# A four-layer decoder on one core: when and from which queue layer 0's expert weights are loaded

## The reference

```python
logits = x @ router_weight.T + router_bias            # [4096, 16]
top_val, top_idx = top_k(logits, 4); softmax(top_val)
gate_up = einsum('th,ehd->etd', x, gate_up_proj) + gate_up_proj_bias   # 256 -> 512 per expert
gate, up = gate_up[..., ::2], gate_up[..., 1::2]      # clipped at 7
out = einsum('etd,edh->eth', (up + 1) * gate * sigmoid(1.702 * gate), down_proj) + down_proj_bias
```

## Time and profile before

| | |
|---|---|
| median of 3 runs | 3678.72 us (3677.7 to 3682.36) |
| profiled execution, first to last instruction | 3689.2 us |
| phase_norms to the end of phase_experts0 | 588 to 1435 us of it |
| TensorE busy over the whole span | 2870.5 us (78%) |
| DMA over the whole span | 386.10 MB, mean 105 GB/s |

### The profile page before, as it was taken

One profiled execution on the slowest core, in us unless ns is written; L12 is line 12 of the kernel. 1 busy time (PEld: TensorE's weight loads), 2 busy tenths in 40 slices (PEclk: granted clock), 3 DMA queues, 4 the chain that ended last, 5 costly groups with the idle time before them and its releaser, 6 DMA issues. The chain is left out here.

```text
span 3689.2 us, 60303 instructions
## 1 busy us (share of the span) xinstructions
PE 2870.5 (78%) x20178; PEld 1835.6 (50%) x20178; DVE 2185.6 (59%) x4954; ACT 1479.2 (40%) x3032; POOL 1095.9 (30%) x1490
## 2 busy tenths in 40 slices
PE   5388884476699995559957698999989649999993
PEld 4223332332355553423323486454568538888782
DVE  7689993577577776634468687888868620000003
ACT  5267772154222224659945454222245211111110
POOL 2111110177233335512269543000034441111110
PEclk7599996599899997569978899999989659999996
DMA  8766644299522223378600252000044221111204
GB/s 261 177 116 119 122 107 140 69 367 361 175 80 80 79 81 133 128 126 128 114 1 1 91 170 65 1 1 1 1 140 143 87 62 56 48 55 50 85 28 137
DMA packets 261609, 386.10 MB, mean 105 GB/s; under 512 B 56865, under 2 KB 188942, under 8 KB 261056
## 3 DMA queue, kind: packets, MB, share of 16 engines
q1 hardware_dynamic: 234480, 312.50, 31.7%
q0 software_dynamic: 25152, 68.22, 5.3%
q10 hardware_dynamic: 1680, 1.57, 0.2%
HBM read 227.49 MB, written 160.24 MB: 105 GB/s over the span
## 5 line engine op out<-in xcount | busy, mean ns | idle before, releaser
L3125 POOL DMA_INDIRECT rows_out<-e_out,e_tr_dest x224 | 234.9, 1048 | 875.9 <-DVE e_out L3755 514.1
L1195 ACT ACTIVATE a_pt<-a_psS 128x512 f32<-128x512 f32 x512 | 277.5, 595 | 155.5 <-PE a_psS L1093 151.1
L3755 DVE COPY e_out<-e_psD 128x512 f32<-128x512 f32 x40 | 27.7, 692 | 496.3 <-PE e_psD L3723 496.1
L1217 DVE TENSOR_REDUCE a_mx_sb<-a_psM 128x4 f32<-128x1024 f32 x256 | 293.1, 1215 | 18.9 <-PE a_psM L1076 17.7
L3523 PE MATMUL e_psG<-e_wgu,e_yT 128*128 x576 | 275.1, 600 | 25.8 <-ACT e_yT L3551 23.2
L1107 PE MATMUL a_psV<-a_pt,a_vt 128*18 128x256 f32 x4096 | 292.2, 387 | 2.0 <-issue 1.6
L3723 PE MATMUL e_psD<-e_w,e_hT 128*128 128x256 f32 x1280 | 293.3, 389 | 0.0
L3712 PE MATMUL e_psH<-e_yT,e_w 128*128 128x256 f32 x1280 | 285.4, 381 | 1.6 <-issue 0.8
L3655 ACT ACTIVATE e_hT<-e_psH 128x512 f32<-128x512 f32 x160 | 95.5, 597 | 456.4 <-PE e_psH L3712 453.1
L3723 PEld LDWEIGHTS e_psD<-e_w,e_hT 128*128 128x128 f32 x1280 | 248.2, 196 | 34.2
L3712 PEld LDWEIGHTS e_psH<-e_yT,e_w 128*128 128x128 f32 x1280 | 244.8, 191 | 35.8 <-issue 2.1
(11 more groups left out here) (428 smaller groups left out, 6110.2 us busy)
## 6 DMA issues: line engine op xcount, KB each, us to landing
kbd<-e_bgu SPq DMA_DIRECT2D x64, 512.0 KB
cr_kbd<-kbd SPq DMA_DIRECT2D x64, 512.0 KB, 3.4
rows_in<-zeros POOLq DMA_DIRECT2D x36, 522.0 KB, 6.6
e_xin<-rows_in SPq DMA_DIRECT2D x144, 128.0 KB
vbd<-e_bd SPq DMA_DIRECT2D x64, 272.0 KB
cr_vbd<-vbd SPq DMA_DIRECT2D x64, 272.0 KB, 2.7
cq_rows<-rows_out SPq DMA_DIRECT2D x32, 512.0 KB, 5.9
e_w<-in_L_ffn_w_dram SPq DMA_DIRECT2D x16, 1024.0 KB, 7.6
```

The costliest lines, as they stand in the source:

```text
L1195: act.activation(pt[:, probs(t, h), b, :, :], psS[:, unit(t, h, b) % S_BANKS, :].rearrange("p (k c) -> p k c", k=KC), ACT.Exp, scale=scale ...
L1217: dve.tensor_reduce(mx[:, t % 2, :, h, :], psM[:, k % 2, :, :].rearrange("p b (f c) -> p b f c", f=2), AX_X, ALU.max).then_inc(ring_read, 1)
L3125: pool.indirect_dma_start(out=self.rows_out[0:limit, :], out_offset=bass.IndirectOffsetOnAxis(ap=self.dest[:, t:t + 1], axis=0), in_=rows, ...
```

## The change

- `phase_norms` issues no loads any more.
- `phase_project` issues the router's weight and bias first, and behind them on the same queue `load_up`: the 16 loads of the first weights and the load of the first bias (12 MB).
- `KeysValues` uses the room of the second weights `e_wd` (seen as [128, 16, 512]) in place of the first bias's room; the second bias's room as before.
- `late` is gone from `phase_scatter`. At the start of `phase_experts0` ScalarE's queue issues `load_down`: the second weights in four loads of four experts each (1 MB, 1,024 pieces of 1 KB), and the second bias (2 MB), before ScalarE's first copy.
- TensorE and VectorE wait at the start for the first weights and bias alone; TensorE waits for all of `e_wd` before its first product with it, VectorE for the second bias before its first addition of it.

```diff
-def phase_norms(core, name, prefetch=None):
+def phase_norms(core, name):
...
-            if prefetch is not None:
-                @block.sync
-                def _(sp):
-                    prefetch(sp)
...
@@ phase_project
                     sp.dma_start(b[:, :], bias.rearrange("(a n) -> a n", a=1).broadcast_to([P, E])).then_inc(bias_loaded, 16)
+                if prefetch is not None:
+                    prefetch(sp)
...
@@ phase_scatter
                     pairs.sync(sp)
-                    late(sp)
...
+class Experts0:
+    PARTS = 4
...
+    def rooms(self):
+        return self.wd[:, :, :, :].rearrange("p e k d -> p e (k d)"), self.bd
...
+    def load_up(self, sp):
+        for e in range(self.E):
+            sp.dma_start(self.wgu[:, e, :, :], self.gate_up[e].rearrange("(k p) f -> p k f", p=P)).then_inc(self.up_loaded, 16)
+        sp.dma_start(self.bgu[:, :, :], self.gate_up_b.rearrange("(a e) f -> a e f", a=1).broadcast_to([P, self.E, self.D2])).then_inc(self.up_loaded, 16)
...
+    def load_down(self, eng):
+        n = self.E // self.PARTS
+        for m in range(self.PARTS):
+            eng.dma_start(self.wd[:, m * n:(m + 1) * n, :, :],
+                          self.down[m * n:(m + 1) * n].rearrange("e (k p) d -> p e k d", p=P)).then_inc(self.down_loaded, 16)
+        eng.dma_start(self.bd[:, :, :], self.down_b.rearrange("(a e) f -> a e f", a=1).broadcast_to([P, self.E, self.D])).then_inc(self.bias_loaded, 16)
...
@@ phase_experts0
-                pe.wait_ge(loaded, 16 * (2 * E + 2))
+                pe.wait_ge(weights.up_loaded, 16 * (E + 1))
...
                         pe.wait_ge(h_copied, t + 1)
+                        if t == 0:
+                            pe.wait_ge(weights.down_loaded, 16 * weights.PARTS)
...
             @block.scalar
             def _(act):
+                weights.load_down(act)
...
-                dve.wait_ge(loaded, 16 * (2 * E + 2))
+                dve.wait_ge(weights.up_loaded, 16 * (E + 1))
...
                         dve.wait_ge(down_done, t + 1)
+                        if t == 0:
+                            dve.wait_ge(weights.bias_loaded, 16)
```

More of the change, by code:

```diff
@@ L450, in _, with phase_project @@
                 pool.wait_ge(powed, 1)
-def phase_project(core, name, E, result, weight_rows=None, weight_cols=None, bias=None, yT_all=None, squares=None):
+def phase_project(core, name, E, result, weight_rows=None, weight_cols=None, bias=None, yT_all=None, squares=None, prefetch=None):
     nc = core.nc
@@ L2749, in _, with phase_scatter @@
                 c.link(dve.tensor_copy(slot[:, :, :], pos[:, :, :]))
-def phase_scatter(core, name, K, slot, rows_in, limit, mark, prefetch, pairs=None, late=None):
+def phase_scatter(core, name, K, slot, rows_in, limit, mark, prefetch, pairs=None):
     nc = core.nc
@@ L3395, in _ @@
                         dve.tensor_tensor(parts[:, g % 2, 2, :, :], z[:, g % 3, :, :], parts[:, g % 2, 1, :, :], ALU.subtract).then_inc(lo, 1)
-def expert_weights0(core, ctx, gate_up, down):
+class Experts0:
     E, D2, D = 16, 2 * DIM, DIM
[L3401 to L3410, removed]
@@ new lines, in __init__ @@
+    def __init__(self, core, ctx, gate_up, gate_up_b, down, down_b):
+        E, D2, D = self.E, self.D2, self.D
+        self.core, self.gate_up, self.gate_up_b, self.down, self.down_b = core, gate_up, gate_up_b, down, down_b
+        self.up_loaded, self.down_loaded, self.bias_loaded = (core.sem("e0_" + k) for k in ("ul", "dl", "bl"))
+        self.wgu = core.sb(ctx, "e0_wgu", [P, E, KC, D2], F32)
+        self.bgu = core.sb(ctx, "e0_bgu", [P, E, D2], F32)
+        self.wd = core.sb(ctx, "e0_wd", [P, E, KC, D], F32)
@@ new lines, in hold_bias @@
+    def hold_bias(self, ctx):
+        self.bd = self.core.sb(ctx, "e0_bd", [P, self.E, self.D], F32)
+    def rooms(self):
[4 more added lines that the diff above has]
+        sp.dma_start(self.bgu[:, :, :], self.gate_up_b.rearrange("(a e) f -> a e f", a=1).broadcast_to([P, self.E, self.D2])).then_inc(self.up_loaded, 16)
@@ L3438, in expert_weights3, with phase_experts0 @@
     return (w1s, w2s, w_loaded), prefetch
-def phase_experts0(core, rows_in, rows_out, expert_of, wgu, wd, bgu, bd, loaded):
+def phase_experts0(core, rows_in, rows_out, expert_of, weights):
     OUTS = 3
     nc = core.nc
-    E, D2, D = 16, 2 * DIM, DIM
+    E, D2, D = weights.E, weights.D2, weights.D
+    wgu, bgu, wd, bd = weights.wgu, weights.bgu, weights.wd, weights.bd
     GROUP0 = 8
@@ L3794, in flamingo_decoder @@
             with ExitStack() as c1:
-                (wgu, wd, loaded), prefetch = expert_weights0(core, c1, a["L0_ffn_gate_up_proj"], a["L0_ffn_down_proj"])
-                phase_norms(core, "n1", prefetch)
+                experts = Experts0(core, c1, *(a["L0_ffn_" + k] for k in ("gate_up_proj", "gate_up_proj_bias", "down_proj", "down_proj_bias")))
+                phase_norms(core, "n1")
                 with ExitStack() as c2:
                     logits = core.sb(c2, "logits0", [P, TILES, 16], F32)
-                    phase_project(core, "l0", 16, logits, weight_rows=a["L0_ffn_router_weight"], bias=a["L0_ffn_router_bias"])
+                    phase_project(core, "l0", 16, logits, weight_rows=a["L0_ffn_router_weight"], bias=a["L0_ffn_router_bias"],
+                                  prefetch=experts.load_up)
                     phase_slots(core, "s0", 16, 4, logits, weight, slot, f_gate(0), expert_of=expert_of)
                 with ExitStack() as c2:
-                    biases, prefetch_bias = expert_biases0(core, c2, a["L0_ffn_gate_up_proj_bias"], a["L0_ffn_down_proj_bias"], loaded)
+                    experts.hold_bias(c2)
                     with ExitStack() as c3:
-                        pairs = KeysValues(core, c3, "kv", *biases, ctxT, key_weights, kbd, vbd)
-                        phase_scatter(core, "sc0", 4, slot, rows_in, D0, MARK0, None, pairs, prefetch_bias)
-                    phase_experts0(core, tiles_in, rows_out, expert_of, wgu, wd, *biases, loaded)
+                        pairs = KeysValues(core, c3, "kv", *experts.rooms(), ctxT, key_weights, kbd, vbd)
+                        phase_scatter(core, "sc0", 4, slot, rows_in, D0, MARK0, None, pairs)
+                    phase_experts0(core, tiles_in, rows_out, expert_of, experts)
             phase_combine_split(core, "cq", 4, weight, rows_out, q_pieces)
```

## The result

The changed kernel takes 3655.45 us (median of 4 runs, 3654.51 to 3656.38), the kernel before, in the same session, 3680.54 us: a ratio of 0.9927, interval 0.9911 to 0.9944, or 25.1 us less. In a later session the two stood at 3665.02 and 3693.22 us, 0.9914 (0.9888 to 0.994).

The account below looks back on a forecast made before the run. Two stage borders were taken to wait for loads: the router behind 12 MB of weights, the experts behind 6 MB of biases. 16.7 + 0 + 9.3 = 26.0 us less than 3678.7 gives 3652.7 us; own range 3649 to 3657, overall 3645 to 3663.

Parts of the forecast that it names:

- Part 1: Norms to router: with the router's loads ahead of 12 MB, TensorE starts at 611.4 instead of 628.09 us, 16.7 us less.
- The cover: Router's projection: the 12 MB land beside it by 648 us, 42 us before the scatter's first loads, at no cost.
- Part 2: Scatter: keys and values use other rooms, the stage stays bound by its transfers; no gain or loss.
- Part 3: Scatter to experts: the wait for the biases goes and the first product comes at 952.7, not 961.96 us; 9.3 us less.
- sign for the first product: Experts' start: the next profile would show the first product 9 to 13 us after the block's start, 20.9 before.
- Tile 1's rows: Experts' start: 2,304 token packets take equal turns with the weights' packets at 367 GB/s; rows in at 949.4 us.
- the hold of tile 1's issue: Experts' start: SyncE's 14.96 us hold before issuing tile 1, behind tags and 6 MB, goes with an empty queue.
- ScalarE's issues: Experts' start: five load issues before ScalarE's first copy, the fifth going at 948.0 us, hidden with 4 us to spare.
- the tokens' wait for all 6 MB: Rival at the experts' start: tokens still wait for all 6 MB; 17.6 us less in all, 3661 us, 20%.
- the tokens pass at once: Rival at the experts' start: tokens, 0.3 MB against 6, are not delayed; 30.2 us less in all, 3648.5 us, 13%.
- the loss by ScalarE's queue: Rival at the experts' start: ScalarE held at its issues makes the kernel slower, 3686 us at 100 GB/s, 2%.
- The clock: Experts' start: TensorE's clock, 0.50 before and in the first products, was expected to start the same; no gain counted.

Follow-up runs that it names:

- e2: Changed kernel, but SyncE issues each load of tags one tile later, behind tile 1's rows; 3662.6 us against 3691.07, ratio 0.9928.
- e12: Changed kernel without the load of the second weights (output wrong) and with the tags behind tile 1's rows; 3658.87 us, one run, against 3693.22.
- e9: Changed kernel, router's loads then first weights issued in the norms, second weights and bias by GpSimd, that bias in four parts; 3662.88 us against 3693.22, ratio 0.992.
- e10: Changed kernel, router's loads issued in the norms ahead of the first weights, tags behind tile 1's rows; 3665.19 us against 3693.22, ratio 0.9923.
- e7: Changed kernel, but SyncE issues the second weights and bias ahead of tile 0's rows, in place of ScalarE; 3669.77 us against 3681.09, ratio 0.9967.
- e5: Changed kernel with tags behind tile 1's rows, and second weights and bias issued by GpSimd; 3662.18 us against 3681.09, ratio 0.9946.
- e3: Changed kernel, but GpSimd issues the second weights and bias in place of ScalarE; 3673.07 us against 3691.07, ratio 0.996.
- e1: Changed kernel, but the first weights and bias are issued in the norms again, ahead of the router's loads; 3678.96 us against 3691.07, ratio 0.9968.

## Why the prediction was right, and where it was not

**Part 1, 16.7 us: right.** The wait shrank by 17.6 us and a new one of 0.8 (VectorE for the router's bias) came: 16.8. The load took 1.6 us, not 2.5; the bias, which the prediction did not price, took most of that back. The 12.6 MB were in at 638.4 us (618.69 + 19.7), 34.6 us after the first issue at 603.8, at 364 GB/s: the near end of the 34 to 38 us reckoned. The cover held: B is 0.7 longer, which is the bias, and nothing else.

**Part 2, nothing: right.** Same rate, same share. The scatter came to 234.3 us, 0.6 less than before where 0.85 was expected; its own spread of 7 us allows no more. The rooms were not changed alone in any run.

**Part 3, 9.3 us: the mechanism right, the size too large by 4.1.** Direct reading: 20.9 - 16.3 = 4.6 us, with the 0.6 above 5.2. The prediction's own sign for the first product, 9 to 13 us after the block's start, was missed, by 3.3 us. Two terms were mis-sized. *Tile 1's rows* were put at 9.1 us after the block's start and were turned at 13.0: the prediction let 2,304 packets pass turn by turn at 367 GB/s, and while the tags were under way the stretch moved 298 and 303 GB/s (921.7 to 925.7 and on to 929.7 us). It also said that the hold of tile 1's issue goes with an empty queue; what stood in it were SyncE's own tags, and the issue was held for 4.4 us. e2 shows 7.7 of the 13.0 us to be the tags. The Trainium skill's round of the queues, packet by packet ("DMA: Bandwidth & Descriptors", section "Queues, rings and completion order"), would make few large packets beside a load dearer than many small ones; e12 (8.4 us) and e2 (5.3 us) agree, without isolating it, and e9, where four times smaller packets brought a row 1.1 us sooner and not 3 to 5, it does not explain. *ScalarE's issues* ended at 9.7 us, 7.7 estimated, and stayed hidden behind the rows, by 2.8 us; in e2 and e10 they are the next to be waited for. The Trainium skill's other sentence (same page, section "Issuing engines are not separate DMA queues": a second issuer saves issue time only) does not hold here as strictly as it is put: e7 issues the same loads from SyncE, and tile 0 comes 17.4 us later than changed, of which 8.4 are issue time. That the loads of several engines interleave, as the same section says, agrees: the changed kernel turned tiles 0 and 1 at 2.7 and 13.0 us, while the 6 MB of ScalarE's queue were in at 22.2; the section does not leave all 6 MB in the tokens' way, as the prediction took it to.

**What none of the terms had.** The prediction measured part 3 at the first product. The table shows a better mark: from the first second-product to the next phase are 466.8 to 468.2 us in all fourteen profiles, whatever came before, while the first product says little (in e5 it is 10.4 us ahead of the changed kernel's, and the phase ends 3.7 us behind it). TensorE can't go on without tiles 2 to 4. In the changed kernel their rows are nearly in time (the longest wait is 0.55 us); where an edit brought tile 1 sooner, a later tile was waited for instead, 2.97 us in e2, 3.21 in e3, 12.11 in e5. By that mark the change gives 31.96 - 27.12 = 4.8 us, of which 3.9 arrive at the phase's end.

**The total.** 26.0 predicted; 25.1 measured by the medians, 21.3 by the stages. The stages are the sharper reading: 3678.7 - 21.3 = 3657.4 us, just above the forecast's own range of 3649 to 3657. That the median lies nearer is in part luck: to the 21.3 us of the stages it adds 3.8 that no stage of the change shows, and they make up for most of the oversized term. Of the rivals, the tokens' wait for all 6 MB did not come (tile 0 and 1 were turned long before the bias landed), nor did the tokens pass at once; the loss by ScalarE's queue did not come either, its 9.7 us of issues cost nothing here. The clock stayed at 1.2 GHz until the first product, as said.

## What to carry to other kernels

Put a small load that is waited for ahead of the large ones that are not, in the same queue; that is worth what is still to be moved of the large ones when the small one is waited for (17 us here); issuing everything earlier in the old order gave 4 (e1). When a large load starts together with a stream of small ones, count the stream's small packets and what lies behind them, several tiles deep, and mark the gain at the point from which the cadence is steady, not at the first result (here the first second-product). An edit that only brings the first result forward can cost more than it gives.

## What the runs showed of the hardware

- 2,048 tags of 20 bytes landed in 3.0 us where GpSimd's loads followed 0.2 us behind them (e3), in 11.8 us beside ScalarE's 1 KB packets, and in 20.6 us where GpSimd's packets, 5 KB each on average, were ahead of them (e5).
- 128 KB of rows, issued right behind another 128 KB, were turned 8.4 us after the block's start beside 2 MB in 16 KB rows (e12), 5.3 beside 6 MB that began with 1 KB rows (e2).
- An issue right behind the 2,048 tags in the same queue was held for 4.4 us (changed kernel).
- After a wait of 3.21 us, which began at a granted clock of 1.00, TensorE's next product ran at 0.50 and took 3.25 us (e3); after a wait of 1.44 us the clock was still 1.00 and the product took 1.91 us (e9).
- Five issues of 6 MB held ScalarE for 9.7 us, SyncE for 8.4 (e7), GpSimd for 4.2 (e3).
- One stage of the same program, layer 3's router and scatter, took 118 us in one session's four profiles, 123 to 124 in another's and 125 to 126 in a third's; a difference of that size between two profiles is no effect of an edit elsewhere.
